# The order of steps in a two-layer, two-stream pipeline: no empty slots, the first layer two tiles ahead of the second, and two buffers for its output

## The chip, the cores and the metric

The kernel runs on one core of one Trainium2 chip. The metric is the device time of that core in microseconds (us). Three runs of the kernel before gave 3565.03, 3568.47 and 3568.79 us; the median is 3568.47 us. The engines are TensorE (PE: matmuls; PEld is its weight load), VectorE (DVE), ScalarE (ACT), GpSimd (POOL), and SyncE (SP), which here issues the DMAs.

## The reference

The input x is 8 sequences of 1024 tokens of 256 features. A layer norm gives xn; the output is x + A(xn) + F(xn). A is a linear attention with a second-order Taylor feature map, and comes first in the program. F is a transformer of two layers, and it is the part that the change touches:

```
for l in range(2):                      # F
    h = shift_token(x)                  # second half of the features from the token before
    q, k, v = split(h @ wqkv[l])        # 8 heads of 64
    q, k = rotary_xpos(l2norm(q) * qs, l2norm(k) * ks)
    o = local_attention(q, k, v)        # windows of 128, each looks at the one before too
    x = x + o @ wo[l]
    h = layer_norm(shift_token(x))
    a, g = split(h @ w1[l] + b1[l])     # 682 each
    x = x + (a * gelu(g)) @ w2[l] + b2[l]
```

Tile `it` of layer 1 needs only tile `it` of layer 0's output and what layer 1 kept of tile `it - 1` (keys, values, one shifted row).

## The kernel before, in words

The Taylor part (`taylor_block`) ends at about 917 us. The rest is `transformer_block`. It treats the 8 sequences as two streams `s` of 4 sequences each; a stream is 32 tiles (`ROUNDS`) of 128 tokens. A **step** is one tile of one layer of one stream, a tuple `(n, s, l, it)`: its number `n` in the order of work, stream, layer and tile. There are 2 x 2 x 32 = 128 steps.

The work runs in **slots**. Slot `j` takes five steps at once, each at another stage of its life, as `steps_at(j)` returns them:

- `nxt` = step at `j + 1`: for a layer-1 step, PE transposes layer 0's output `xmid` (`x_T`) and ACT copies it into `hT` (`copy_hT`); for a layer-0 step nothing, since `hT` is loaded by DMA;
- `cur` = step at `j`: the projections K, Q and V (`project`), norms and rotation, transposes of the heads (`heads_T`), and scores;
- `att` = step at `j - 1`: exponentials, transposes of the probabilities (`prob_T`), `attend`, `out_project`;
- `nrm` = step at `j - 2`: the residual sum `x1` (`add_attention`), the token shift by DMA, the layer norm, `hn_T`;
- `ffn` = step at `j - 3`: `up`, GELU and gate, `down`, and the sum `add_ffn` into `xmid` (layer 0) or `yout` (layer 1).

Each engine has one `slot` function that lists the work of the five stages in a fixed order, and `run` calls it for every slot from -1 to `SLOTS + 2`. Where `steps_at` gives `None`, that stage's work is left out. Engines wait for each other by semaphores which count steps, so the order of steps is what `step_of(j)` says. All loops are unrolled when the program is built.

`step_of` before: slot 0 holds (stream 0, layer 0, tile 0) and slot 2 (stream 1, layer 0, tile 0); slots 1 and 3 are empty. From slot 4 on, four slots make a round `r`: (0, layer 0, tile r), (0, layer 1, tile r-1), (1, layer 0, tile r), (1, layer 1, tile r-1). The last four slots, 128 to 131, are empty, (0, layer 1, tile 31), empty, (1, layer 1, tile 31). That makes 132 slots for 128 steps, and three more (132 to 134) in which the last steps run out. A slot is called *full* here when `cur`, `att`, `nrm` and `ffn` all are there: slot 5 and slots 7 to 127. Each empty slot also leaves a hole in the `att`, `nrm` and `ffn` work of the three slots behind it.

`middle_of(step)` gives the number of the layer-0 step whose output a layer-1 step reads; `x_T` on PE waits for it on the semaphore `x2_ready`.

Names in the profile: `f_ps` is PSUM, L1362 `project`, L1367 `heads_T`, L1389 and L1396 scores, L1407 and L1411 `prob_T`, L1426 and L1436 `attend`, L1447 `out_project`, L1348 and L1349 `x_T`, L1454 `hn_T`, L1470 and L1475 `up`, L1482 `down`, L1170 the copy of the normalised tile `hnT` on DVE, L1103 `unit_k` on DVE. On SP: L917 loads part of `hT` for a layer-0 step, L939 keeps the values of a tile for the next one.

Of the kernel before, what the change touches and what calls it, by code (L numbers as in the profile page):

```python
# [15 lines left out]
ALU = mybir.AluOpType  # L16
# [3 lines left out]
P = 128  # L20
DIM = 256
# [11 lines left out]
SLOTS = 6  # L33
# [673 lines left out]
def transformer_block(nc, PAIRS, x, xn_d, attn_d, xnT_d, wqkv_s, wo, w1, b1, w2, ln, id_s, rot, masks_s, last_stored, out):  # L707
# [6 lines left out]
    with ExitStack() as ctx:  # L714
# [12 lines left out]
        ps = ctx.enter_context(nc.psum_tensor("f_ps", [P, 8, 512], F32))  # L727

        SCORES = (0, 1, 2, 3)
        XT, HNT, K, V, Q, KT, QT, OT, WO, DOWN = 4, 5, 4, 5, 5, 4, 5, 6, 7, 3  # L730
# [12 lines left out]
        def per_stream(name, shape):  # L743
            return [sb(f"{name}{s}", shape) for s in range(2)]

        xin = per_stream("xin", [P, DIM])
# [3 lines left out]
        vw = per_thread("vw", [P, 4, INNER])  # L750
        x1 = per_thread("x1", [P, DIM + P])
        xsh = per_thread("xsh", [P, P])
        xmid = per_stream("xmid", [P, DIM])
        yout = per_stream("yout", [P, DIM])
        xb = per_stream("xb", [P, DIM])
        qk = sb("qk", [P, 2 * HEADS, HD])
# [37 lines left out]
        xT_ps = sem("xT_ps")  # L794
# [37 lines left out]
        x1_ready = sem("x1_ready")  # L832
# [18 lines left out]
        STREAMS = range(2)  # L851
        PAIRS_OF_HEADS = [(0, 2), (1, 3), (4, 6), (5, 7)]
        MIDDLE, OWN, OLDEST, NEWEST = range(4)
        ROUNDS = PAIRS * TILES
        SLOTS = 4 * ROUNDS + 4
        block = ctx.enter_context(nc.Block())

        def thread_step(r, c):

            r, c = r + c // 4, c % 4  # L860
            return 4 * r + c - 2, c // 2, c % 2, r - c % 2

        def step_of(j):
            if j in (0, 2):
                return j // 2, j // 2, 0, 0
            if j < 4 or j >= SLOTS or j in (SLOTS - 4, SLOTS - 2):
                return None
            if j >= SLOTS - 4:
                return 4 * ROUNDS - 2 + (j - SLOTS + 3) // 2, (j - SLOTS + 3) // 2, 1, ROUNDS - 1
            return thread_step(j // 4, j % 4)  # L870

        FIRST_FFN = 3

# [13 lines left out]
            return not isinstance(count, int) or count > 0  # L887

        def middle_of(step):

            n, s, l, it = step
            if isinstance(it, int) and it in (0, ROUNDS - 1):
                return s if it == 0 else 4 * ROUNDS - 6 + 2 * s
            return n - 5

        def chances(h):
            k = h // 2 % 2
# [173 lines left out]
        def _(dve):  # L1071
# [61 lines left out]

            def add_attention(step):
                n, s, l, it = step
                xprev = xin[s] if l == 0 else xmid[s]
                if l == 0:
                    dve.wait_ge(xn_in[s], 16 * it + 16)
                if some(it):
                    dve.wait_ge(carried[s][l], 16 * it)  # L1140
                dve.wait_ge(wo_ps, n + 1)
                v.tensor_tensor(x1[s][l][:, 0:DIM], ps[:, WO, 0:DIM], xprev[:, :], ALU.add).then_inc(x1_ready, 1)

            def row_statistics(step):
                n, s, l, it = step
# [37 lines left out]
            def add_ffn(step):  # L1183
                n, s, l, it = step
                if l == 0:
                    dve.wait_ge(down_ps, n + 1)
                    v.tensor_tensor(xmid[s][:, :], ps[:, DOWN, 0:DIM], x1[s][l][:, 0:DIM], ALU.add).then_inc(x2_ready, 1)
                else:
                    if some(it):
                        dve.wait_ge(y_out[s], 16 * it)  # L1190
                    dve.wait_ge(xb_ready[s], 2 * it + 2)
                    dve.wait_ge(down_ps, n + 1)
                    v.tensor_tensor(yout[s][:, :], ps[:, DOWN, 0:DIM], xb[s][:, :], ALU.add).then_inc(x2_ready, 1)
# [146 lines left out]
        def _(pe):  # L1340
            mm, tr = nc.tensor.matmul, nc.tensor.transpose

            def x_T(step):
                n, s, l, it = step
                if l == 0:
                    return
                pe.wait_ge(x2_ready, middle_of(step) + 1)
                tr(ps[:, XT, 0:P], xmid[s][:, P:DIM], id_s[:, :])  # L1348
                tr(ps[:, XT, P:2 * P], xmid[s][:, 0:P], id_s[:, :]).then_inc(xT_ps, 1)  # L1349

            def project(step, i, b, done):
                n, s, l, it = step
# [274 lines left out]
```

## Time and profile before

| | |
|---|---|
| runs, us | 3565.03, 3568.47, 3568.79 (median 3568.47) |
| profiled execution, us | 3566.8 |
| its span, first to last instruction, us | 3564.7 |
| mean granted TensorE clock | 0.989 |
| PE matmul busy | 3441.9 us, 97% |
| PE weight load busy | 2425.4 us, 68% |
| DVE / ACT / POOL busy | 2619.5 / 2667.9 / 1332.4 us |
| TensorE's share of the chain that ended last | 71% |

The page shows the span in 40 slices of 89 us with the busy tenths of each engine. The transformer part begins at 922.97 us with the first projection. The stretches that matter are short beside the span (one slot is about 20 us), so they are read from the busy times by stretch and from the timeline, not from the page.

### The profile page before, as it was taken

How to read it: one execution, taken by the hardware profiler on the slowest of the kernel's cores; microseconds unless marked ns; L12 is line 12 of the kernel's file. 1: busy time of each engine (PE TensorE's matmuls, PEld its weight loads, DVE VectorE, ACT ScalarE, POOL GpSimd, SP SyncE). 2: the span in 40 equal slices, each digit the busy share in tenths (PEclk: the TensorE clock that was granted, in tenths of full speed). 3: DMA queues.
4: the chain of work that ended last, by engine and by line, in shares of the span. 5: the costliest groups of instructions: out<-in, count | busy, mean ns of one | idle time of the engine just before them, and what ended most of it. 6: DMA issues, size and time to landing. Idle time of an engine off the chain costs nothing.

```text
span 3564.7 us, 87646 instructions
## 1 busy us (share of the span) xinstructions
PE 3441.9 (97%) x32608; PEld 2425.4 (68%) x32608; DVE 2619.5 (73%) x8000; ACT 2667.9 (75%) x5724; POOL 1332.4 (37%) x1194
## 2 busy tenths in 40 slices
PE   7999999999689999999999999999999999999997
PEld 3433344433468787878788787778788787878786
DVE  3665555654578888888888888888887888888874
ACT  6788877788367777777777777777777777777774
POOL 1221212211244444444444444444444444444432
PEclk9999999999799999999999999999999999999999
DMA  6655675546322222222222222222222222222210
GB/s 156 143 136 128 131 155 135 119 96 112 107 56 68 67 65 72 61 72 63 71 66 70 65 64 73 61 72 63 71 66 68 67 64 73 61 71 64 71 45 22
DMA packets 289671, 293.21 MB, mean 82 GB/s; under 512 B 40928, under 2 KB 221280, under 8 KB 288736
## 3 DMA queue, kind: packets, MB, share of 16 engines
q1 hardware_dynamic: 289248, 287.62, 34.1%
q8 instruction: 260, 4.26, 0.5%
q14 instruction: 163, 1.34, 0.1%
HBM read 104.77 MB, written 58.73 MB: 46 GB/s over the span
## 4 chain that ended last, share of the span: by engine, by line
PE 71%; issue 2%; DVE 1%; POOL 1%; ACT 0%; DMA 0%; SPq 0%; POOLq 0%; DVEq 0%; ACTq 0%
PE f_ps L1362 18%; PE f_ps L1470 16%; PE f_ps L1482 9%; PE f_ps L1447 6%; PE f_ps L1426 4%; PE f_ps L1367 3%; PE f_ps L1389 3%; PE f_ps L1407 3%; PE f_ps L1436 2%; PE f_ps L1396 2%; PE f_ps L1475 2%; PE f_ps L1411 2%; PE f_ps L1454 1%; PE f_ps L1348 0%; POOL turned L1033 0%
## 5 line engine op out<-in xcount | busy, mean ns | idle before, releaser
L1033 POOL TENSOR_TENSOR turned<-qk,rot 128x256 f32<-128x256 f32 x512 | 407.2, 816 | 1287.8 <-ACT qk L1245 1258.8
L1362 PE MATMUL f_ps<-wqkv_s,hT 128*128 128x512 f32 x1536 | 707.2, 596 | 9.5 <-DMA hT<-xnT_dram 5.5
L1470 PEld LDWEIGHTS f_ps<-hnT,w_s 128*128 128x128 f32 x5120 | 596.3, 193 | 70.9 <-issue 61.6
L1470 PE MATMUL f_ps<-hnT,w_s 128*128 128x128 f32 x5120 | 597.7, 276 | 10.3 <-DVE hnT L1170 10.3
L1113 DVE CUSTOM_DVE_ANT_0 pr<-f_ps,masks_s 128x192 f32<-128x192 f32 x1024 | 326.3, 355 | 355.2 <-PE f_ps L1396 353.2
L545 ACT ACTIVATE weights<-t_ps,four_s 128x1024 f32<-128x1024 f32 x576 | 580.4, 1302 | 7.6 <-PE t_ps L653 7.2
L1278 ACT ACTIVATE pr<-pr,nmax,rnorm 128x192 f32<-128x192 f32 x1024 | 545.2, 535 | 46.6 <-DVE nmax L1120 46.6
L1362 PEld LDWEIGHTS f_ps<-wqkv_s,hT 128*128 128x128 f32 x1536 | 276.8, 190 | 276.0 <-issue 188.0
L1130 DVE TENSOR_SCALAR pr<-pr,rsum 128x192 f32<-128x192 f32 x1024 | 439.9, 491 | 9.0
L392 DVE SCALAR_TENSOR_TENSOR weights<-weights,causal_s 128x512 f32<-128x512 f32 x192 | 163.9, 868 | 279.3 <-ACT weights L545 278.9
L1482 PE MATMUL f_ps<-w_s,act_u 128*128 128x256 f32 x1536 | 352.7, 379 | 0.0
L670 PE MATMUL t_ps<-weights,vals 128*32 128x512 f32 (+3 forms) x3072 | 308.6, 497 | 18.4 <-DVE weights L392 13.1
L653 PE MATMUL t_ps<-qkT 96*128 96x512 bf16 (+3 forms) x1536 | 308.9, 332 | 13.7 <-ACT weights L545 8.0
L1040 POOL TENSOR_TENSOR rnorm<-ssq,f_mhalf 128x8 f32<-128x8 f32 x128 | 254.5, 1988 | 159.5 <-DVE ssq L1090 159.5
L1482 PEld LDWEIGHTS f_ps<-w_s,act_u 128*128 128x128 f32 x1536 | 281.9, 190 | 33.5 <-issue 0.5
L1267 ACT ACTIVATE kT<-f_ps 128x512 f32<-128x512 f32 x128 | 76.4, 597 | 295.9 <-PE f_ps L1367 295.9
L653 PEld LDWEIGHTS t_ps<-qkT 96*128 96x128 bf16 x1536 | 111.7, 98 | 272.7 <-ACT weights L545 174.9
L1302 ACT ACTIVATE act_u<-f_ps,b_s 128x128 f32<-128x128 f32 x640 | 205.1, 365 | 112.3 <-PE f_ps L1475 89.1
L286 POOL TENSOR_TENSOR yT<-yT,den 128x1024 f32<-128x1024 f32 x24 | 62.8, 2615 | 539.7 <-DVE den L335 539.7
L1447 PE MATMUL f_ps<-fwo_s,oT 128*128 128x256 f32 x1024 | 242.8, 380 | 2.7 <-ACT oT L1291 2.6
L1080 DVE TENSOR_TENSOR cosine<-qk,rot 128x512 f32<-128x512 f32 x256 | 208.9, 816 | 20.1 <-ACT qk L1245 19.9
L1180 DVE SCALAR_TENSOR_TENSOR act_u<-f_ps,b_s,act_u 128x128 f32<-128x128 f32 (+1 forms) x768 | 208.8, 340 | 17.7 <-ACT act_u L1302 13.5
(119 smaller groups left out, 6312.6 us busy)
## 6 DMA issues: line engine op xcount, KB each, us to landing
vw<-vw SPq DMA_DIRECT2D x628, 128.0 KB, 2.5
qkT<-parts_dram SPq DMA_DIRECT2D x384, 128.0 KB, 5.8
kT<-kT SPq DMA_DIRECT2D x124, 256.0 KB, 2.7
parts_dram<-parts SPq DMA_DIRECT2D x64, 384.0 KB, 2.9
xnT_dram<-xnT SPq DMA_DIRECT2D x8, 1025.0 KB, 4.8
xs<-x_dram SPq DMA_DIRECT2D x8, 1024.0 KB, 7.9
xn_dram<-xn SPq DMA_DIRECT2D x8, 1024.0 KB, 5.4
attn_dram<-ao SPq DMA_DIRECT2D x8, 1024.0 KB, 10.5
```

The lines of the kernel that those rows point to most:

```text
L545: a.activation(weights[:, w:w + 2, :], ps[:, bank:bank + 2, :], ACT.Square, bias=four_s[:, :]).then_inc(squared, 1)
L653: last = mm(ps[:, unit_bank(n) + k, o:o + 512 - c], qkT[g % 2][:, 1, h, j * P:(j + 1) * P], qkT[g % 2][:, 0, h, half * 512 + c:(half + 1) ...
L670: last = mm(ps[h * VP:(h + 1) * VP, half, c:512], vals[:, j, g * GH + h, :], weights[:, GH * (i % RING) + h, o:o + 512 - c], start=(j == 0 ...
L1033: g.tensor_tensor(turned[:, heads, f], qk[:, heads, z], sines, ALU.mult).then_inc(done, 1)
L1040: g.tensor_tensor(rnorm[:, HEADS:], ssq[:, HEADS:], mhalf[:, HEADS:], ALU.pow).then_inc(knorm_ready, 1)
L1113: last = v.tensor_tensor_reduce(out=chances(h), in0=ps[:, SCORES[p], k * 256:k * 256 + BAND], in1=mask_of(it)[:, HALF - k * HALF:HALF - k ...
L1130: last = v.tensor_scalar_mul(chances(h), chances(h), rsum[:, h:h + 1])
L1278: last = a.activation(chances(h), chances(h), ACT.Exp, bias=nmax[:, h:h + 1], scale=rnorm[:, h:h + 1], accum_out=psum[:, h:h + 1])
L1362: last = mm(ps[:, b, :], rows, wqkv_s[:, l, c, i * INNER:(i + 1) * INNER], start=(c == 0), stop=(c == KC - 1))
L1447: last = mm(ps[:, WO, 0:DIM], oT[:, c, :], wo_s[:, l, c, :], start=(c == 0), stop=(c == INNER // P - 1))
L1470: last = mm(ps[:, UP[j // 2], o:o + P], w1_s[:, l, c, half * FULL + j * P:half * FULL + j * P + P], hnT[:, c, :], start=(c == 0), stop=(c ...
L1482: last = mm(ps[:, DOWN, 0:DIM], act_u[:, j, :], w2_s[:, l, j, :], start=(j == 0), stop=(j == FB - 1))
```

## The change

`step_of` becomes a lookup in a list, `ORDER`, with 128 entries for 128 slots. The list begins with layer 0 of tiles 0 and 1 of both streams, and then alternates layer 0 of tile r + 2 with layer 1 of tile r; for the last two tiles only layer 1 is left. So the order is (stream, layer, tile): (0,0,0), (1,0,0), (0,0,1), (1,0,1), (0,0,2), (0,1,0), (1,0,2), (1,1,0), ... , (0,1,30), (1,1,30), (0,1,31), (1,1,31). Since layer 0 is now two tiles ahead, its output `xmid` has two buffers per stream, picked by `it % 2`. In the middle a stream's step of one layer still comes four slots after that layer's step before it. At the start three such pairs have a distance of two slots (slots 0 and 2, 1 and 3, 2 and 4) and one has three (3 and 6); at the end three have two (123 and 125, 124 and 126, 125 and 127) and one has three (121 and 124).

```diff
-        xmid = per_stream("xmid", [P, DIM])
+        xmid = per_stream("xmid", [P, 2, DIM])
...
-        SLOTS = 4 * ROUNDS + 4
+        SLOTS = 4 * ROUNDS
...
-        def thread_step(r, c):
-
-            r, c = r + c // 4, c % 4
-            return 4 * r + c - 2, c // 2, c % 2, r - c % 2
+        AHEAD = 2
+        ORDER = [(s, 0, it) for it in range(AHEAD) for s in STREAMS]
+        for r in range(ROUNDS):
+            for s in STREAMS:
+                if r + AHEAD < ROUNDS:
+                    ORDER.append((s, 0, r + AHEAD))
+                ORDER.append((s, 1, r))
+        NUMBER = {step: n for n, step in enumerate(ORDER)}
 
         def step_of(j):
-            if j in (0, 2):
-                return j // 2, j // 2, 0, 0
-            if j < 4 or j >= SLOTS or j in (SLOTS - 4, SLOTS - 2):
-                return None
-            if j >= SLOTS - 4:
-                return 4 * ROUNDS - 2 + (j - SLOTS + 3) // 2, (j - SLOTS + 3) // 2, 1, ROUNDS - 1
-            return thread_step(j // 4, j % 4)
+            return (j,) + ORDER[j] if 0 <= j < SLOTS else None
...
         def middle_of(step):
-
             n, s, l, it = step
-            if isinstance(it, int) and it in (0, ROUNDS - 1):
-                return s if it == 0 else 4 * ROUNDS - 6 + 2 * s
-            return n - 5
+            return NUMBER[s, 0, it]
...
-                xprev = xin[s] if l == 0 else xmid[s]
+                xprev = xin[s][:, :] if l == 0 else xmid[s][:, it % 2, :]
...
-                    v.tensor_tensor(xmid[s][:, :], ps[:, DOWN, 0:DIM], x1[s][l][:, 0:DIM], ALU.add).then_inc(x2_ready, 1)
+                    v.tensor_tensor(xmid[s][:, it % 2, :], ps[:, DOWN, 0:DIM], x1[s][l][:, 0:DIM], ALU.add).then_inc(x2_ready, 1)
...
-                tr(ps[:, XT, 0:P], xmid[s][:, P:DIM], id_s[:, :])
-                tr(ps[:, XT, P:2 * P], xmid[s][:, 0:P], id_s[:, :]).then_inc(xT_ps, 1)
+                tr(ps[:, XT, 0:P], xmid[s][:, it % 2, P:DIM], id_s[:, :])
+                tr(ps[:, XT, P:2 * P], xmid[s][:, it % 2, 0:P], id_s[:, :]).then_inc(xT_ps, 1)
```

The line numbers of the changed kernel are 5 lower behind `middle_of` (L1362 becomes L1357, and so on).

On PE, behind the scores of the very first step, the kernel before has the whole attention of that step by itself (`prob_T`, `attend`, `out_project`), and then the projections of the next one:

```order
L1407 MATMUL f_ps<-id_s,pr 128x128 x8
L1411 MATMUL f_ps<-id_s,pr 128x128 x4
L1426 MATMUL f_ps<-pT,vw 64x128 x8
L1436 MATMUL f_ps<-pT,vw 64x64 x16
L1447 MATMUL f_ps<-fwo_s,oT 128x256 x4
L1362 MATMUL f_ps<-wqkv_s,hT 128x512 x6
L1367 MATMUL f_ps<-id_s,qk 128x128 x8
```

At the same place on PE the changed kernel has the projections of the second step first, and the attention of the first step among its transposes and scores:

```order
L1357 MATMUL f_ps<-wqkv_s,hT 128x512 x6
L1402 MATMUL f_ps<-id_s,pr 128x128 x8
L1406 MATMUL f_ps<-id_s,pr 128x128 x4
L1362 MATMUL f_ps<-id_s,qk 128x128 x8
L1421 MATMUL f_ps<-pT,vw 64x128 x8
L1431 MATMUL f_ps<-pT,vw 64x64 x16
L1384 MATMUL f_ps<-kT,qT 64x128 x4
L1391 MATMUL f_ps<-kT,qT 64x64 x4
```

The second step has moved up by one slot, so that slot 1 holds the two steps' work together; the third step (tile 1 of stream 0) follows in slot 2, and from slot 3 on every slot is full.

The last rows of PE in the kernel before: `up`, attention and `down` of slot 132, and then the last step's `hn_T`, `up` and `down` with no other work between:

```order
L1470 MATMUL f_ps<-hnT,w_s 128x128 x20
L1475 MATMUL f_ps<-hnT,w_s 106x128 x2
L1407 MATMUL f_ps<-id_s,pr 128x128 x8
L1411 MATMUL f_ps<-id_s,pr 128x128 x4
L1482 MATMUL f_ps<-w_s,act_u 128x256 x6
L1426 MATMUL f_ps<-pT,vw 64x128 x8
L1436 MATMUL f_ps<-pT,vw 64x64 x16
L1447 MATMUL f_ps<-fwo_s,oT 128x256 x4
L1454 MATMUL f_ps<-id_s,hn 128x128 x2
L1470 MATMUL f_ps<-hnT,w_s 128x128 x20
L1475 MATMUL f_ps<-hnT,w_s 106x128 x2
L1482 MATMUL f_ps<-w_s,act_u 128x256 x6
```

The last rows of PE in the changed kernel, from the `down` of slot 128 on (L1421 and L1431 are `attend`, L1449 `hn_T`, L1442 `out_project`, L1465 and L1470 `up`, L1477 `down`):

```order
L1477 MATMUL f_ps<-w_s,act_u 128x256 x6
L1421 MATMUL f_ps<-pT,vw 64x128 x8
L1431 MATMUL f_ps<-pT,vw 64x64 x16
L1449 MATMUL f_ps<-id_s,hn 128x128 x2
L1442 MATMUL f_ps<-fwo_s,oT 128x256 x4
L1465 MATMUL f_ps<-hnT,w_s 128x128 x20
L1470 MATMUL f_ps<-hnT,w_s 106x128 x2
L1477 MATMUL f_ps<-w_s,act_u 128x256 x6
L1449 MATMUL f_ps<-id_s,hn 128x128 x2
L1465 MATMUL f_ps<-hnT,w_s 128x128 x20
L1470 MATMUL f_ps<-hnT,w_s 106x128 x2
L1477 MATMUL f_ps<-w_s,act_u 128x256 x6
```

Between the last `out_project` and the last `hn_T` there now stand an `up` and a `down` of the step before.

## Rows read from the trace of the kernel before

**Rows 1.** The page: span, busy time of PE, and its 40 slices
```profile
span 3564.7 us, 87646 instructions
PE   7999999999689999999999999999999999999997
```

**Rows 2.** Busy time by stretch (us, busy and count per engine, clock, DMA): slots 7 to 126
```profile
1038.20:3444.00 2405.80, 2405.68 (x25321) 1930.62 (x25320) 1980.70 (x6600) 1821.04 (x4441) 1066.56 (x960) 1.00 0.26 67
```

**Rows 3.** Groups by line, the same stretch (busy, mean ns, idle before): projections
```profile
L1362 PE MATMUL f_ps<-wqkv_s,hT 128*128 128x512 f32 x1440 | 660.1, 594 | 0.1
```

**Rows 4.** Busy time by stretch: slots 0 to 6, one row each
```profile
922.97:940.40 17.43, 12.90 (x84) 7.28 (x84) 6.86 (x15) 4.56 (x9) 10.43 (x16) 0.70 0.97 361
940.40:952.10 11.70, 7.00 (x68) 5.56 (x69) 4.43 (x25) 6.52 (x20) 0.00 (x0) 0.66 0.33 83
952.10:966.80 14.70, 10.56 (x87) 5.91 (x85) 9.11 (x27) 5.10 (x11) 7.49 (x7) 0.84 0.15 37
966.80:983.90 17.10, 13.94 (x125) 12.86 (x125) 6.68 (x29) 8.92 (x25) 0.00 (x0) 0.84 0.17 42
983.90:999.50 15.60, 11.45 (x89) 6.97 (x87) 9.60 (x29) 6.29 (x12) 7.54 (x7) 0.78 0.17 43
999.50:1019.50 20.00, 19.93 (x208) 15.87 (x209) 14.51 (x50) 15.91 (x42) 7.04 (x6) 1.00 0.21 51
1019.50:1038.20 18.70, 14.69 (x158) 10.41 (x157) 13.91 (x50) 11.06 (x31) 8.02 (x7) 0.91 0.24 60
```

**Rows 5.** Busy time by stretch: slots 128 to 132, then the last step alone
```profile
3464.10:3478.80 14.70, 13.10 (x129) 11.84 (x129) 7.99 (x33) 8.78 (x24) 0.56 (x1) 1.00 0.19 50
3478.80:3495.30 16.50, 15.65 (x144) 11.90 (x142) 11.12 (x29) 7.61 (x15) 10.16 (x9) 1.00 0.11 31
3495.30:3513.20 17.90, 14.36 (x128) 13.07 (x128) 7.57 (x34) 10.47 (x29) 0.00 (x0) 0.90 0.08 22
3513.20:3527.50 14.30, 10.19 (x85) 6.25 (x83) 9.30 (x22) 5.77 (x10) 8.91 (x9) 0.81 0.10 24
3527.50:3544.10 16.60, 13.52 (x134) 11.55 (x127) 7.51 (x34) 9.76 (x27) 0.00 (x0) 0.96 0.03 9
3544.10:3551.80 7.70, 0.69 (x2) 0.29 (x2) 3.64 (x9) 0.00 (x0) 1.97 (x3) 0.84 0.03 8
3551.80:3564.70 12.90, 9.79 (x56) 9.13 (x56) 2.24 (x7) 1.99 (x6) 0.00 (x0) 0.83 0.03 10
```

**Rows 6.** Timeline of PE (start, us, instructions, idle before): slots 0 and 6
```profile
922.97 6.12 PE L1362 MATMUL f_ps<-wqkv_s,hT 128*128 128x512 f32 x8 [5.52 <-DMA hT<-xnT_dram]
...
1019.50 3.60 PE L1362 MATMUL f_ps<-wqkv_s,hT 128*128 128x512 f32 x8
1024.12 1.98 PE L1362 MATMUL f_ps<-wqkv_s,hT 128*128 128x512 f32 x4 [1.03 <-ACT qk L1245]
...
1030.40 1.97 PE L1367 MATMUL f_ps<-id_s,qk 128*128 128x128 f32 x8 [2.98 <-DVE qk L1103]
```

**Rows 7.** Timeline of SP's queue and of PE in slots 0 and 3
```profile
934.25 0.45 SPq L917 DMA_DIRECT2D hT<-xnT_dram  x1
...
969.27 6.12 PE L1470 MATMUL f_ps<-hnT,w_s 128*128 128x128 f32 x40 [2.44 <-DVE hnT L1170]
```

**Rows 8.** One line's instructions (L917, up to 1000 us): its loads' landings
```profile
DMA to landing us min/median/max: 2.0/2.5/9.6
```

**Rows 9.** One line's instructions (L939, 1100 to 3000 us): its copies' landings
```profile
DMA to landing us min/median/max: 2.2/2.6/4.1
```

**Rows 10.** Timeline of PE in the last slots
```profile
3530.65 4.73 PE L1470 MATMUL f_ps<-hnT,w_s 128*128 128x128 f32 x40 [2.34 <-DVE hnT L1170]
...
3550.34 0.69 PE L1454 MATMUL f_ps<-id_s,hn 128*128 128x128 f32 x2 [6.26 <-DVE hn L1162]
...
3551.85 6.76 PE L1470 MATMUL f_ps<-hnT,w_s 128*128 128x128 f32 x40 [0.82 <-DVE hnT L1170]
...
3558.88 2.76 PE L1482 MATMUL f_ps<-w_s,act_u 128*128 128x256 f32 x12
```

More of the change, by code:

```diff
@@ L1141, in add_attention @@
                 dve.wait_ge(wo_ps, n + 1)
-                v.tensor_tensor(x1[s][l][:, 0:DIM], ps[:, WO, 0:DIM], xprev[:, :], ALU.add).then_inc(x1_ready, 1)
+                v.tensor_tensor(x1[s][l][:, 0:DIM], ps[:, WO, 0:DIM], xprev, ALU.add).then_inc(x1_ready, 1)
             def row_statistics(step):
```

## The prediction, made before the changed kernel had run

> **What bounds the kernel now.** I read the page first, for where PE is not busy; then the busy times by stretch; then the timeline at both ends of the transformer part. The page shows 9 or more tenths of PE in nearly every slice. The exceptions are the first slice, two around the start of the transformer part (6 and 8 tenths), and the last [rows 1]. In between, from 1038.2 to 3444.0 us, PE has matmuls for 2405.68 of 2405.80 us, at a granted clock of 1.00, while DVE is busy for 1980.70 and ACT for 1821.04 us [rows 2]. In that stretch 1440 projection matmuls ran [rows 3]; a step has 12 of them (8 for K and Q, 4 for V, as slot 6 shows them [rows 6]), so it is 120 slots of 2405.8 / 120 = 20.05 us. PE's own work sets the full slot; nothing else ends late there.
>
> At the ends it is otherwise. Slots 0 to 6 have 90.5 us of PE work in 115.2 us, and in all but the full slot 5 the granted clock was only 0.66 to 0.91 [rows 4]. The stretches behind slot 127 have 77.3 us in 100.6 us [rows 5]. There the waits are chains between engines: PE idles 2.98 us in slot 6 until DVE has the unit keys, and 6.26 us before the last `hn_T` [rows 6, 10]. So 24.7 us of idle time lie at the start and 23.3 at the end. The two stretches do the work of 128 - 121 = 7 full slots, 140.3 us, and have 167.8 us of PE busy for it: the other 27.5 us are matmuls at the lower clock. Together 75 us; the rest of the transformer part has no idle time to give.
>
> **The change part by part.** It removes no arithmetic: 128 steps before and after, with the same instructions each. It changes how many slots are full. The sum goes over the whole transformer part, from 922.97 us to the end of the span at 3564.7 us.
>
> Before: slots 0 to 6 take 17.43 + 11.70 + 14.70 + 17.10 + 15.60 + 20.00 + 18.70 = 115.2 us [rows 4]; slots 7 to 127 take 3464.1 - 1038.2 = 2425.9 us, 121 slots of 20.05; and what follows takes 14.7 + 16.5 + 17.9 + 14.3 + 16.6 + 7.7 + 12.9 = 100.6 us [rows 5]. The total is 2641.7 us.
>
> After, slot by slot:
>
> Slot 0 is as before, 17.4 us. It has one step's `cur` work, and it begins when its DMA lands [rows 6].
>
> Slot 1 has `cur` of the second step and `att` of the first. The trace has no such slot. From above it is bounded by nothing overlapping: slot 1 of before, which is that attention alone, and slot 2, which is that `cur` alone, 11.7 + 14.7 = 26.4 us [rows 4]. From below it is bounded by PE never idle: slot 6 holds the same matmuls and a few transposes more, and has 14.7 us of PE work [rows 4]; less half a microsecond for those, 14.2 us. The nearest row is slot 6 itself, 18.7 us: it has `cur`, `att` and `nrm` and no `ffn`. Its critical part is from the K projection at 1019.50 to the transposes of the heads at 1030.40, 10.9 us [rows 6], through ACT, POOL and DVE, and that chain doesn't change in slot 1. I take 18.7 less 1.0 us for the work of `nrm` that isn't there: 17.7 us.
>
> Here the clock matters. Slot 0's eight K and Q matmuls took 6.12 us against 3.60 in slot 6, and the clock granted over slots 0 and 1 was 0.70 and 0.66 of the upper level, a mixture of 1.2 and 2.4 GHz [rows 4, 6]. In slot 1 of before PE had idled about 3 us before the first transposes; in the changed kernel it goes from the scores straight to projections. If the lower level lasted through K and Q, slot 1 would be 2.5 us longer, 20.2 us; the bounds above hold either. The Trainium skill, "TensorE: Matmul & The Clock Gate", section "What's actually happening", says that the throttled state is the default and that activity releases it. By that rule the busier slot 1 gets the upper level early and the 17.7 us stand; by slot 0's row alone it would be 20.2 us. The trace agrees with the rule in that all 120 full slots had 1.00.
>
> Slot 2 has `cur`, `att` and `nrm` and no `ffn`, exactly as slot 6: 18.7 us, and not under its 14.7 us of PE work. From slot 3 on all slots are full, to slot 127: 125 slots of 20.05 = 2506.1 us. The order of kinds in them (stream 0 layer 0, stream 0 layer 1, stream 1 layer 0, stream 1 layer 1) is that of before for slots 4 to 123, so every engine's list in a slot is the same, SP's and POOL's too. `x_T` had no wait in any full slot of before (PE's idle sum is 0.12 us), and now its input is four slots older. Slots 0 to 4 hold five layer-0 steps in a row and slots 123 to 127 five layer-1 steps; their PE work differs only by `x_T`, which was in the mean.
>
> Behind slot 127: slot 128 has `att`, `nrm` and `ffn`, as slot 128 had before: 14.7 us, less the `x_T` that it had, 14.4. Slot 129 has `nrm` of the last step beside `ffn` of the one before. `up` and `down` are 4.9 and 2.6 us at full clock (in slot 132 `up` ran in 4.73 with its 0.4 of edge rows behind it, `down` is 2.76 and overlaps [rows 10]); together with gates in between I take 8.3 us. The chain that gives the last `hn`, 6.3 us in the row of 3550.34, runs beside it and is hidden. Its ends are 7.5 us (PE alone) and 7.5 + 6.3 = 13.8 us (nothing hidden). Slot 130 is the last `ffn`: from `hn_T` at 3550.34 to the end it took 14.4 us, with `up` at the lower clock (6.76 us against 4.73 in slot 132 [rows 10]). Before, PE had idled 6.26 us ahead of it, and now it comes straight from `down`, so I take the upper level: 14.4 - 2.0 - 0.3 = 12.1 us, and 14.4 us as the other end.
>
> The sum: 17.4 + 17.7 + 18.7 + 2506.1 + 14.4 + 8.3 + 12.1 = 2594.7 us, against 2641.7: 47.0 us less. The span would be 3517.7 us and the profiled execution (2.1 us above its span) 3519.8 us. The profiled execution of before, 3566.8 us, is 1.7 us under the median of the runs, so for the median I expect 3568.5 - 47.0 = 3521.5, say 3522 us.
>
> The second `xmid` buffer costs nothing in time: the same instructions with another offset. The first layer-0 tiles want their DMAs sooner, while the weights still load. The last `hT` load of the third step was issued at 934.25 us and landed at most 9.6 us later [rows 7, 8], by 944 us; PE wants it at the start of slot 2, at 922.97 + 17.4 + 17.7 = 958 us. It is hidden by 14 us, and the loads of `w1` and `w2` that `up` waits for in slot 3 had landed before too, as PE's `up` in slot 3 of before started at 969.27 us and waited for DVE's `hnT` and not for them [rows 7]; its place is now 976.8 us or later.
>
> **What the distance of two could cost.** At both ends a thread's step follows its predecessor by two slots in place of four. What the next step needs from the one before are kept keys, kept values and the carried row. The values are the tightest: SP issues them behind `attend`, which in a full slot ends some 16 us in, they land 2.6 us later in the median and at most 4.1 [rows 9], three copies; ACT's copy of the next V comes about 10 us into the slot after. That leaves some 8 us. Queued behind such a wait would be ACT's copies of the probabilities, and behind them PE's `attend`. I cost it at nothing, and at 5 us for each of the six pairs at a distance of two if SP is late by being stuck in front of another wait.
>
> **The rivals.**
>
> *Close pairs wait.* Six times 5 us: 3522 + 30 = 3552 us. For it: SP's queue is in order and it waits for `hn_ready` and `v_ready` before it reaches the values. Against: all of these come earlier in the slot than `attend`.
>
> *Less overlap at the ends.* Slot 1 at 22, slot 129 at 12 and the last `up` at the lower clock: 4.3 + 3.7 + 2.3 = 10 us more, 3532 us. This is the forecast with its unknown terms near the upper ends.
>
> *Slower: the full slot gets longer.* PE is at 1.00 of the clock for 2406 us, and no empty slot interrupts it in that stretch. If PE, now dense from slot 1 to slot 129, were granted a lower clock, the price is on 125 slots: at 0.98, 20.05 / 0.98 = 20.46, or 51 us in all, and the time would be 3573 us. The point from which it decides is 47 / 125 = 0.38 us a slot, a granted clock of 0.981. Against it speaks that the clock never fell in 120 full slots in a row [rows 2]; five more won't differ.
>
> *The change doesn't do what it says.* It gains at one end only, because the other has a chain that I don't see. Idle time and lower clock are split about evenly between the ends (24.7 and 23.3 us idle), so one end alone gives half of 47 us: 3545 us. For it: slots 1 and 2 are not in the trace as they will be. Against: slots 6, 128 and 132 are nearly the new slots 2, 128 and 129.
>
> **How the numbers follow.** The forecast, 3522 us, has 0.80; its own range is 3515 to 3530. Less overlap at the ends, 3532 us, has 0.10. Close pairs or one end only, 3545 to 3552 us, have 0.04 and 0.02. The slower clock has 0.02. About 0.02 are left for a reason that makes no difference in all. A measurement of this kernel can tell about 0.2%, 7 us, from no change. All cases but the last two are faster by more than that: faster 0.96, same 0.02, slower 0.02. The lower end of the range is from the bounds: slot 1 at 14.2 and slot 2 at 14.7 would take 7.5 us off, so 3514.5; the upper end takes in the 3532 us case. The range is 3515 to 3534 us.
>
> **What would show it.** In the changed kernel's profile, from the first projection: slot 3 should begin 53.8 us in, with its predecessors at 17.4, 17.7 and 18.7 us. The 125 full slots should have a mean of 20.05 us with no idle time of PE and a clock of 1.00. From the end of the last scores (start of slot 128) to the end of the span it should be 35 us, and the wait before the last `hn_T` under 1 us where it was 6.26. If close pairs wait, ACT's copy of V or PE's `attend` shows idle time in slots 2 to 5 or 124 to 127. The prediction is wrong if the full slots' mean moves by more than 0.05 us, or if one end doesn't shrink.

## The result and the profile after

| | before | after |
|---|---|---|
| runs, median (range), us | 3568.07 (3565.03 to 3568.79) | 3518.58 (3517.42 to 3520.59) |
| profiled execution, us | 3566.8 | 3517.4 |
| its span, us | 3564.7 | 3515.6 |
| mean granted TensorE clock | 0.989 | 0.995 |

The ratio is 0.9865, with a 95% interval of 0.9853 to 0.9876: 49.5 us less. Two later sets of runs of the same kernel gave 0.9869 (0.9854 to 0.9884) and 0.9870 (0.9854 to 0.9887), which is 46.2 us (3567.55 to 3521.38) and 47.2 us (3567.90 to 3520.72). The forecast was 3522 us, its range 3515 to 3534.

The page of the changed kernel, span, PE and granted clock in 40 slices:

```profile
span 3515.6 us, 87647 instructions
PE   7999999999699999999999999999999999999999
PEclk9999999999899999999999999999999999999999
```

Against [rows 1], one low slice is left near the start of the transformer part where there were two, and the last slice has 9 tenths where it had 7.

The busy time of the engines by stretch (us; busy time and count of PE, PEld, DVE, ACT, POOL; clock; DMA share; GB/s). The rows are slot 0, slot 1, slot 2, slots 3 to 127, slot 128, slot 129 up to `hn_T`, and the rest:

```profile
922.22:938.13 15.91, 11.13 (x84) 6.18 (x85) 6.67 (x15) 4.49 (x9) 10.32 (x16) 0.82 0.97 361
938.13:955.42 17.29, 13.31 (x157) 8.91 (x153) 12.95 (x48) 11.64 (x33) 7.02 (x6) 0.98 0.46 115
955.42:973.79 18.37, 14.36 (x156) 10.08 (x155) 13.63 (x49) 10.63 (x29) 8.01 (x7) 0.91 0.24 60
973.79:3481.10 2507.31, 2506.98 (x26379) 2011.18 (x26377) 2061.30 (x6877) 1896.87 (x4631) 1107.85 (x999) 1.00 0.26 66
3481.10:3495.89 14.79, 12.97 (x127) 11.65 (x127) 8.21 (x33) 8.13 (x22) 1.98 (x3) 1.00 0.05 15
3495.89:3503.39 7.50, 7.50 (x58) 7.14 (x57) 3.52 (x13) 1.98 (x6) 1.96 (x3) 1.00 0.04 10
3503.39:3515.60 12.21, 8.14 (x59) 7.24 (x57) 3.30 (x10) 1.98 (x6) 0.00 (x0) 1.00 0.06 21
```

These rows answer to [rows 2, 4, 5]. The account of the transformer part:

| stretch | before | forecast | after |
|---|---|---|---|
| slots that fill the pipeline | 115.2 (0 to 6) | 53.8 (0 to 2) | 51.6 |
| full slots | 2425.9 (121 of 20.05) | 2506.1 (125 of 20.05) | 2507.3 (125 of 20.06) |
| behind slot 127 | 100.6 | 34.8 | 34.5 |
| sum | 2641.7 | 2594.7 | 2593.4 |

The sum fell by 48.3 us; the other 0.8 us of the span's 49.1 are ahead of it, in the Taylor part that the change doesn't touch: the first projection started at 922.22 and not at 922.97 us. PE's idle time in the full slots is 0.33 us in 2507. In the two ends PE's idle time fell from 48.0 us (24.7 and 23.3) to 18.7 us (86.1 us less 67.4 busy). What the ends take over the pure work of 128 slots (128 x 20.05 = 2566.4 us) fell from 75 to 27 us, so the rest of the gain, some 19 us, is shorter busy time of PE for the same work: matmuls that no longer run at the lower clock level.

What became of the chain ahead of the last `hn_T` is in the timeline (start, us, instructions, idle time before and what ended it). PE runs `up` and `down` of the step before, DVE normalises the last tile beside them:

```profile
3495.89 4.63 PE L1465 MATMUL f_ps<-hnT,w_s 128*128 128x128 f32 x40
...
3499.19 0.29 DVE L1146 BATCH_NORM_STATS2 st<-xsh 128x6 f32<-128x128 f32 x1 [2.26 <-DMA xsh<-x]
...
3500.80 2.76 PE L1477 MATMUL f_ps<-w_s,act_u 128*128 128x256 f32 x12
...
3502.55 0.33 DVE L1157 TENSOR_SCALAR hn<-xsh,mv,rstd 128x128 f32<-128x128 f32 x1
3503.39 0.38 PE L1449 MATMUL f_ps<-id_s,hn 128*128 128x128 f32 x2
...
3504.80 4.73 PE L1465 MATMUL f_ps<-hnT,w_s 128*128 128x128 f32 x40 [1.03 <-DVE hnT L1165]
```

The last half of `hn` is done at 3502.88 us, half a microsecond before PE is free for it. The 6.26 us of idle time of [rows 10] are gone, and the last `up` runs in 4.73 us, at the upper clock level, where it took 6.76.

The waits of ACT (who waited for whom: us in total, times, longest) show what the close pairs cost, first in slots 3 to 127, then in slots 0 to 2:

```profile
ACT kT L1262 <- PE f_ps L1362: 284.3, 125, 2.6
ACT vw L1255 <- PE f_ps L1357: 129.6, 125, 1.3
...
ACT kT L1262 <- PE f_ps L1362: 8.8, 3, 3.3
ACT vw L1255 <- PE f_ps L1357: 4.2, 3, 1.4
```

The copies of K and V waited for PE in all 128 steps, never for a DMA that keeps the keys or values of the step before. The first close pair is slots 0 and 2. SP issues the last of its three copies of values in slot 1, and ACT's copy of the next V stands in slot 2:

```profile
953.74 0.60 SPq L936 DMA_DIRECT2D vw<-vw  x1
...
962.12 0.60 ACT L1255 ACTIVATE vw<-f_ps 128x512 f32<-128x512 f32 x1 [1.41 <-PE f_ps L1357]
```

The three copies of this line up to 1000 us landed at most 3.6 us after issue, so by 957.3 us at the latest: nearly 5 us in hand, where the prediction had estimated some 8.

### The profile page after: what moved, and what is told of

It is laid out like the page before. It is cut to its first block, busy times and chain, and to the rows that moved or that the text cites. A ratio compares the mean times of both kernels' runs of the same rounds, so it can differ in the third digit from the quotient of the medians.

```text
span 3515.6 us, 87647 instructions
## 1 busy us (share of the span) xinstructions
PE 3421.8 (97%) x32608; PEld 2412.3 (69%) x32608; DVE 2617.1 (74%) x8000; ACT 2663.9 (76%) x5724; POOL 1330.7 (38%) x1194
## 3 DMA queue, kind: packets, MB, share of 16 engines
q1 hardware_dynamic: 289248, 287.62, 34.8%
## 4 chain that ended last, share of the span: by engine, by line
PE 72%; DVE 1%; POOL 0%; ACT 0%; issue 0%; DMA 0%; SPq 0%; DVEq 0%; POOLq 0%
PE f_ps L1357 18%; PE f_ps L1465 16%; PE f_ps L1477 9%; PE f_ps L1442 6%; PE f_ps L1421 4%; PE f_ps L1362 3%; PE f_ps L1384 3%; PE f_ps L1402 3%; PE f_ps L1431 2%; PE f_ps L1391 2%; PE f_ps L1470 2%; PE f_ps L1406 2%; PE f_ps L1449 1%; PE f_ps L1343 0%; DVE pr L1108 0%
## 5 line engine op out<-in xcount | busy, mean ns | idle before, releaser
L1357 PE MATMUL f_ps<-wqkv_s,hT 128*128 128x512 f32 x1536 | 706.8, 595 | 9.4 <-DMA hT<-xnT_dram 5.6
L1465 PEld LDWEIGHTS f_ps<-hnT,w_s 128*128 128x128 f32 x5120 | 591.7, 192 | 63.0 <-issue 59.8
L1465 PE MATMUL f_ps<-hnT,w_s 128*128 128x128 f32 x5120 | 592.5, 275 | 2.5 <-DVE hnT L1165 2.5
L1357 PEld LDWEIGHTS f_ps<-wqkv_s,hT 128*128 128x128 f32 x1536 | 276.7, 190 | 273.8 <-issue 186.0
L1477 PE MATMUL f_ps<-w_s,act_u 128*128 128x256 f32 x1536 | 352.7, 379 | 0.0
L1477 PEld LDWEIGHTS f_ps<-w_s,act_u 128*128 128x128 f32 x1536 | 281.9, 190 | 33.0
L1442 PE MATMUL f_ps<-fwo_s,oT 128*128 128x256 f32 x1024 | 242.4, 380 | 0.3 <-ACT oT L1286 0.3
## 6 DMA issues: line engine op xcount, KB each, us to landing
attn_dram<-ao SPq DMA_DIRECT2D x8, 1024.0 KB, 10.3
```

What stands on the lines that cost most here:

```text
L1357: last = mm(ps[:, b, :], rows, wqkv_s[:, l, c, i * INNER:(i + 1) * INNER], start=(c == 0), stop=(c == KC - 1))
L1442: last = mm(ps[:, WO, 0:DIM], oT[:, c, :], wo_s[:, l, c, :], start=(c == 0), stop=(c == INNER // P - 1))
L1465: last = mm(ps[:, UP[j // 2], o:o + P], w1_s[:, l, c, half * FULL + j * P:half * FULL + j * P + P], hnT[:, c, :], start=(c == 0), stop=(c ...
L1477: last = mm(ps[:, DOWN, 0:DIM], act_u[:, j, :], w2_s[:, l, j, :], start=(j == 0), stop=(j == FB - 1))
```

## The experiments

All were compared with the kernel before on the same chip. The changed kernel itself ran again beside the last five of them, not beside the first four; those are set against its 3518.6 us of the result. There it took 3521.38 and 3520.72 us, both within what had been expected (3518.6 within 3 us, and 3517 to 3523). Two theories stood against each other. **Holes**: an empty slot costs what PE idles and what clock it loses in it and in the three slots behind, whose work is missing by turns; nothing else in the change moves time. **Lead**: the two tiles of distance, or the second buffer, take a wait away. Three helpers stand in the edits: `PLACED` is `ORDER` with empty slots, and `step_of(j)` looks a step up in it; `NUMBER` gives its number as before.

### Holes back at the end, start dense

```diff
-        SLOTS = 4 * ROUNDS
+        SLOTS = 4 * ROUNDS + 2
...
+        PLACED = ORDER[:-2] + [None, ORDER[-2], None, ORDER[-1]]
```

> The changed kernel (two ahead, two buffers) with two empty slots put back before each of the last two steps, as before had them; the start stays dense. Theory (the time is in the holes): start as in the changed kernel, 51.6 us for slots 0 to 2, then 123 full slots of 20.06, then 100.6 us as the kernel before had behind slot 127: 2619 us against 2593, so 3518.6 + 26 = 3545 us. Rival (the lead of two tiles or the second buffer brings the gain, holes cost nothing because the engines drain at the same pace): 3519 us.

Measured: 3549.46 us (3548.11 to 3550.48), ratio 0.9955 (0.9940 to 0.9970). Its stretches: fill, 123 full slots, and the rest.

```profile
922.21:978.28 56.07, 44.11 (x390) 28.71 (x391) 33.36 (x109) 26.73 (x69) 25.46 (x29) 0.80 0.51 162
978.28:3445.34 2467.06, 2466.73 (x25955) 1978.67 (x25953) 2028.27 (x6767) 1866.26 (x4555) 1087.82 (x981) 1.00 0.26 66
3445.34:3547.40 102.06, 78.70 (x665) 65.34 (x664) 49.90 (x166) 44.40 (x110) 23.10 (x24) 0.88 0.11 29
```

The end is 102.1 us long, where before had 100.6, and the full slots keep their 20.06 us. The lead is there in full and brings nothing. The median was 4 us over the expected 3545 us; in the profile that is the fill, 56.1 us against 51.6, at a granted clock of 0.80. The same instructions stand in those slots: PE is busy for 44.1 us in place of 38.8. The later runs return to this.

### Holes back at the start, end dense

```diff
-        SLOTS = 4 * ROUNDS
+        SLOTS = 4 * ROUNDS + 2
...
+        PLACED = [ORDER[0], None, ORDER[1], None] + ORDER[2:]
```

> The changed kernel with two empty slots put back behind each of the first two steps, as before had them; the end stays dense. Theory: 115.2 us for slots 0 to 6, 123 full slots of 20.06, 34.5 us behind the last full slot: 2617 us, so 3542 us. Rival (lead or buffer): 3519 us. With the other run: the two losses must add up to the whole gain of 49 us, if start and end are independent.

Measured: 3541.85 us (3539.45 to 3542.56), ratio 0.9932 (0.9916 to 0.9949).

```profile
922.27:1037.00 114.73, 89.79 (x810) 64.21 (x811) 64.49 (x217) 57.52 (x141) 40.62 (x43) 0.83 0.33 100
1037.00:3504.10 2467.10, 2466.61 (x25960) 1979.66 (x25958) 2031.26 (x6771) 1868.33 (x4559) 1094.90 (x985) 1.00 0.26 66
3504.10:3538.60 34.50, 28.81 (x240) 26.08 (x240) 14.72 (x56) 11.80 (x33) 3.95 (x6) 1.00 0.05 16
```

The start is nearly that of before (115.2 us), the end that of after (34.5 us). Against 3518.6 us the two losses are 30.9 and 23.3 us, 54.2 us together where the whole gain is 49.5. The 4.7 us too many are about the 4.5 us by which the fill was longer in the profile of the run with end holes. The stretches leave that out. The end holes add 102.1 - 34.5 us and take two full slots away: 27.4 us. The start holes give 114.7 - 51.6 less two full slots: 23.0 us. That is 50.5 us together against the 48.3 of the account above, so they add up within about 2 us, and the end's part is the larger.

### Old order, two buffers

```diff
-        xmid = per_stream("xmid", [P, DIM])
+        xmid = per_stream("xmid", [P, 2, DIM])
```

(and `it % 2` in its four uses; nothing else. The order is that of the kernel before.)

> The kernel before with the second xmid buffer and nothing else of the change (order with four empty slots, one tile ahead). Theory: the buffer by itself moves nothing, 3568 us, full slot 20.05 us. Rival (the buffer frees a wait between the layers, or its shift of the addresses behind it changes durations): away from 3568 by more than 7 us.

Measured: 3566.71 us (3561.71 to 3567.71) against 3565.44 for before in the same set; ratio 1.000 (0.9991 to 1.001). The busy times over the 120 slots of [rows 2]:

```profile
1037.98:3443.90 2405.92, 2405.81 (x25321) 1930.58 (x25320) 1981.76 (x6600) 1821.16 (x4441) 1065.96 (x960) 1.00 0.26 67
```

A slot is 2405.92 / 120 = 20.05 us, as it was. The buffer alone does nothing; it only allows the order.

### One buffer, one tile ahead, two holes

```diff
-        xmid = per_stream("xmid", [P, 2, DIM])
+        xmid = per_stream("xmid", [P, 1, DIM])
...
+        AT = {}
+        for it in range(ROUNDS):
+            for s in STREAMS:
+                AT[4 * it + 2 * s - 1 if it else s] = (s, 0, it)
+                AT[min(4 * it + 4, 4 * ROUNDS - 1) + 2 * s] = (s, 1, it)
+        PLACED = [AT.get(j) for j in range(SLOTS)]    # SLOTS = 4 * ROUNDS + 2
```

> One xmid buffer and layer 0 one tile ahead as before, in the densest order that this allows: slots 0 and 1 hold the first two layer-0 steps, slot 2 is empty, then the alternation, and slot 129 behind (0,1,31) is empty, 130 slots. Theory (a hole costs about 12 us wherever it is, the lead nothing): two holes remain of four, some 100 us at the start to slot 5, 122 full slots, 68.5 us at the end: 2616 us, 3541 us. Rival (the lead of two tiles is what helps): near 3568 us.

Measured: 3544.27 us (3543.92 to 3545.49), ratio 0.9941 (0.9926 to 0.9956). So the step `(0,1,31)` stands in slot 127, the hole behind it is slot 128, and the last step is in slot 129. Fill, 122 full slots, rest:

```profile
920.25:1025.20 104.95, 87.75 (x814) 61.88 (x815) 65.36 (x220) 57.97 (x145) 41.35 (x43) 0.88 0.36 108
1025.20:3471.11 2445.91, 2445.69 (x25743) 1962.60 (x25741) 2014.10 (x6710) 1851.62 (x4516) 1084.62 (x976) 1.00 0.26 66
3471.11:3542.60 71.49, 54.06 (x453) 46.38 (x452) 32.90 (x112) 28.32 (x73) 14.13 (x15) 0.90 0.07 18
```

Two holes fewer than before give 21 us (3565.44 less 3544.27; 19 us by the stretches of the two traces), with the old lead and one buffer: not quite half of the gain. The median is 3 us over the expected 3541 us; the start took 105.0 us where some 100 were expected, and the end 71.5 where 68.5 were. What the second buffer buys is the other two holes, some 26 us (3544.27 less 3518.58).

### A hole in the middle

```diff
-        SLOTS = 4 * ROUNDS
+        SLOTS = 4 * ROUNDS + 1
...
+        PLACED = ORDER[:64] + [None] + ORDER[64:]
```

> The changed kernel with one empty slot put in behind step 63, in the middle of the full slots. Theory (an empty slot costs what PE idles in it and in the three slots behind, whose work is missing by turns, and the clock that it loses there): four holes cost 49 us at the ends, so about 12 us, 3531 us. Rival (in the middle the engines catch up, since PE alone is the bound and the others have a quarter of their time free, and the cost belongs to start and end): under 4 us, 3521 us.

Measured: 3530.73 us (3528.63 to 3533.98); the changed kernel in the same set 3521.38 us. The stretches are slot 63, the hole, the three slots behind it, and the next:

```profile
2178.56:2198.65 20.09, 20.08 (x211) 15.84 (x209) 16.68 (x56) 15.23 (x39) 10.17 (x9) 1.00 0.25 65
2198.65:2213.38 14.73, 12.92 (x126) 11.65 (x127) 8.15 (x33) 8.07 (x21) 0.56 (x1) 1.00 0.30 80
2213.38:2230.06 16.68, 15.83 (x145) 12.09 (x143) 11.35 (x29) 7.91 (x17) 10.16 (x9) 1.00 0.12 32
2230.06:2251.17 21.11, 20.12 (x210) 15.88 (x210) 15.49 (x57) 16.30 (x42) 7.04 (x6) 1.00 0.24 61
2251.17:2270.99 19.82, 15.81 (x157) 11.38 (x156) 13.85 (x50) 11.01 (x31) 8.01 (x7) 0.83 0.29 70
2270.99:2290.91 19.92, 19.92 (x211) 16.02 (x210) 16.52 (x55) 15.06 (x38) 10.17 (x9) 1.00 0.19 51
```

The four slots take 72.3 us for the work of three (60.2 us): 12.2 us for one hole. PE idles for 7.7 us of them (1.8, 0.9, 1.0 and 4.0 us in the four slots), and the other 4.5 us are longer busy time for the same work, 3.4 of them in the last slot, at 0.83 of the clock. The medians differ by 9.4 us and the spans of the two profiles by 10.3: the fill of this run was 3.3 us shorter than that of the changed kernel beside it (52.65 us at 0.87 against 55.90 at 0.80), and its first projection came 1.5 us later. The rival's 4 us is out: the engines do not catch up. The most expensive slot is the last, 19.8 us with no `ffn` in it. PE's work there would be 12.4 us at the upper clock (a full slot's 19.9 less 7.5 of `up` and `down`); it is busy for 15.8 because the granted clock fell to 0.83, and nothing fills the wait for the keys, which ended here:

```profile
2262.07 1.97 PE L1364 MATMUL f_ps<-id_s,qk 128*128 128x128 f32 x8 [2.98 <-DVE qk L1100]
```

An empty slot isn't 20 us lost, nor nothing: it shifts work out of four slots, and in each the chain between the engines is longer than what PE has left.

### Three tiles ahead

```diff
-        AHEAD = 2
+        AHEAD = 3
```

(with three `xmid` buffers and `it % 3`; `xb` moved to other memory to make room.)

> Layer 0 three tiles ahead with three xmid buffers (xb moved to the memory of a table no longer used, to make room), no empty slots. Theory (only holes cost): as the changed kernel, 3519 us within 2 us, since all slots from 3 to 127 are full here too; twice as many pairs of steps follow at a distance of two, and they cost nothing. Rival (pairs at a distance of two wait, or the lead itself helps): away from 3519 us by more than 4 us, slower with idle time of PE in slots 2 to 9 and 118 to 127, or faster.

Measured: 3520.17 us (3517.13 to 3521.79); the changed kernel in the same set 3521.38 (3518.90 to 3523.37). Fill, 125 full slots, rest:

```profile
920.95:973.60 52.65, 40.10 (x390) 26.16 (x391) 33.26 (x109) 26.74 (x69) 25.41 (x29) 0.87 0.52 168
973.60:3480.89 2507.29, 2507.01 (x26379) 2011.24 (x26377) 2061.10 (x6877) 1897.18 (x4631) 1109.88 (x999) 1.00 0.26 66
3480.89:3515.30 34.41, 28.55 (x240) 26.02 (x240) 14.93 (x56) 11.98 (x33) 3.94 (x6) 1.00 0.05 16
```

More lead and more close pairs change nothing that can be measured, in the total, the full slots or the end. The pairs at a distance of two are 10 here (five at either end) against 6 (three at either end), and not twice as many as the text before the run says. The fill of 52.7 us lies between the 51.6 and 55.9 us of the changed kernel's profiles, with the same instructions.

### First loads early

```diff
+                if b + 1 == B:      # in store_attn, ahead of the Taylor part's last store, on SP
+                    for s in range(2):
+                        hT, hT_in = first_hT[s]
+                        rows = xnT_d[s * (B // 2)]
+                        sp.wait_ge(xnT_stored, 16 * (s * (B // 2) + 1))
+                        sp.dma_start(hT[:, 0:P], rows[1, :, 0:P]).then_inc(hT_in, 16)
+                        sp.dma_start(hT[:, P + 1:2 * P + 1], rows[0, :, 1:1 + P]).then_inc(hT_in, 16)
...
-            for s in STREAMS:
-                load_hT(s, 0)
```

> The changed kernel, with the two streams' first hT loads issued at the end of the Taylor part, ahead of its last store, in place of the first thing in the transformer part. PE now idles 5.6 us before the first projection, from the Taylor part's last matmul to the load's landing. Theory (what is left of the gain at the start is the fill, so an earlier first projection moves all behind it): about 3 to 4 us of the 5.6 go, 3515 us. Rival (slot 0 then waits for something else, zeroing by GpSimd or the start of the block): 3518.6 us as the changed kernel.

Measured: 3517.13 us (3514.72 to 3518.72) against 3521.38 for the changed kernel in the same set; ratios to before 0.9859 (0.9843 to 0.9875) and 0.9869 (0.9854 to 0.9884). PE's first projection in its timeline:

```profile
915.47 5.37 PE L1362 MATMUL f_ps<-wqkv_s,first_hT 128*128 128x512 f32 x8 [1.37 <-PEq L62]
```

The wait of 5.6 us became 1.4 us, and the medians differ by the same 4 us. The intervals overlap, so the total alone doesn't prove it; the wait's going is plain in the trace. The fill itself is as it was (55.56 us at 0.82, against 55.90 at 0.80). The 3515 us expected are missed by 2.1 us, as the changed kernel beside it was 2.8 us above the 3518.6 that they were reckoned from.

### PE kept busy in the fill

```diff
+            def keep_warm(count):
+                for _ in range(count):
+                    tr(ps[:, WO, 3 * P:4 * P], id_s[:, :], id_s[:, :])
...
+                if cur and cur[0] == 0:
+                    keep_warm(20)
                 if cur:
                     project(cur, 1, K, k_ps)
...
+                if cur and cur[0] < 3:
+                    keep_warm(14)
                 if cur:
                     pe.wait_ge(k_unit, cur[0] + 1)
```

> The changed kernel with idle-time transposes of the identity on TensorE, into columns of PSUM that nobody reads: 20 ahead of the first projection, while it waits for its load, and 14 ahead of the transposes of the heads in slots 0, 1 and 2, where PE waits about 3 us for VectorE. The three slots of the fill took 51.6 us at a mean granted clock of 0.91 in one run of the changed kernel and 55.9 us at 0.69 to 0.87 in another, with all else equal. Theory (what varies in the fill, and 4 to 9 us of its length, is the clock that PE loses in these waits): the fill's clock goes to 0.95 or more, its length to 46 to 49 us, and the median to about 3514 us, with runs closer together. Rival (the fill is bound by the chain through ScalarE, GpSimd and VectorE, and the extra transposes only get in its way): 3519 to 3524 us.

Measured: 3514.10 us (3511.78 to 3516.02); the changed kernel in the same set 3520.72 (3518.72 to 3522.97). Ratios to before 0.9852 (0.9838 to 0.9867) and 0.9870 (0.9854 to 0.9887). The fill, slots 0 to 2, in one stretch, first of this kernel:

```profile
919.26:968.14 48.88, 40.46 (x432) 27.37 (x433) 33.26 (x109) 26.79 (x69) 25.39 (x29) 0.97 0.55 177
```

Then of the changed kernel, in the profile of its second set of runs, slot by slot, and last its three slots in one stretch in the set of this experiment:

```profile
920.98:938.51 17.53, 13.00 (x85) 7.28 (x85) 6.79 (x15) 4.49 (x9) 10.41 (x16) 0.69 0.99 364
938.51:957.23 18.72, 15.19 (x157) 10.16 (x154) 12.94 (x48) 11.62 (x33) 7.02 (x6) 0.87 0.31 75
957.23:976.88 19.65, 15.64 (x155) 11.20 (x154) 13.62 (x49) 10.62 (x29) 8.01 (x7) 0.83 0.26 65
...
922.50:978.14 55.64, 43.47 (x391) 28.58 (x392) 33.35 (x109) 26.74 (x69) 25.43 (x29) 0.80 0.51 163
```

With 42 transposes more in it, and 20 ahead of it, the fill is 48.9 us at a mean granted clock of 0.97. Without them it was 51.6 us in the first profile of the changed kernel (0.91; 0.82, 0.98 and 0.91 in its slots), 55.9 in the second and 55.6 in the third (both 0.80). Three more kernels of these experiments have the same three slots untouched: 56.1 us at 0.80 with the end holes, and 52.65 at 0.87 both with three tiles ahead and with the hole in the middle. In these six PE's idle time is 12.0 to 12.8 us, and its busy time runs from 38.8 to 44.1 us. So what varies in the untouched fill is how long the matmuls take, with the clock. The transposes take from both: against the third profile idle time fell from 12.2 to 8.4 us and busy time from 43.5 to 40.5, though it holds more work. The chain through the other engines isn't held up by it.

No run of this kernel was as slow as the fastest of the changed kernel beside it (3516.02 against 3518.72), though the intervals of the ratios overlap. Of the 9.9 us between the two profiles' spans the fill explains 6.8. The rest lies in the Taylor part: its last matmul ended at 913.7 us in this profile and at 916.9 in the other, with the same instructions, and the first projection followed 5.5 and 5.6 us later. So the medians' 6.6 us agree with the fill, and the forecast of 3514 us with a fill of 46 to 49 us came out. The runs did not come closer together, as had been expected, but stayed 4.2 us apart with and without the transposes; the end of the Taylor part, which lies between 913.7 and 917.4 us in the profiles, varies as much by itself.

### Both

The two edits above together, with 8 transposes ahead of the first projection in place of 20.

> The same idle-time transposes on top of the early first loads (8 ahead of the first projection, as the wait there is short). Theory: both savings add, since one is ahead of slot 0 and the other in it: 4 to 5 us earlier first projection and 4 to 9 us less fill, about 3510 us. Rival: 3517 us as with the early loads alone.

Measured: 3514.38 us (3513.70 to 3514.88), ratio 0.9853 (0.9839 to 0.9868). They don't add up; the forecast of 3510 us was wrong. The start of the transformer part and the fill in its profile:

```profile
918.37 1.78 PE L1487 MATMUL f_ps<-id_s 128*128 128x128 f32 x8 [1.37 <-PEq L62]
919.94 4.61 PE L1362 MATMUL f_ps<-wqkv_s,first_hT 128*128 128x512 f32 x8
...
919.94:970.90 50.96, 42.91 (x433) 28.73 (x433) 35.22 (x109) 26.86 (x69) 26.79 (x37) 0.91 0.55 178
```

Two things are missing. With the early loads alone the projections began 1.37 us behind the Taylor part; here the eight transposes stand in that place, and the projections begin 1.6 us later. And the fill is 2 us longer than with the warm fill alone, at 0.91 of the clock: the first eight projection matmuls took 4.61 us here, 3.70 with twenty transposes ahead of them, and 5.37 with none and the early loads. That eight were too few for the clock fits this, but isn't shown, since one profile each is all there is. Twenty take the projections' place for longer still (2.4 us in the run above); with early loads they weren't tried. Both kernels, the warm fill and this one, have medians under the changed kernel's.

## Why the prediction was right

**PE sets the full slot, and the order doesn't change it.** Forecast 125 slots of 20.05 us; measured 20.06, and 20.05 to 20.06 in every order tried: one, two or three tiles ahead, with one, two or three buffers. One word of the text before the prediction needs setting right: slot 5 of the kernel before isn't full, since its `nrm` would be the step of the empty slot 3 (its row has 208 matmuls, a full slot 211). The sum doesn't hang on it, as slots 0 to 6 entered it as measured.

**The time lies in the ends.** Start and end holes each put their share back. The prediction took 47.0 us for the four holes; 48.3 came in the profile, and 49.5, 46.2 and 47.2 in the medians of three sets of runs. One hole in the middle costs 12.2 us in its trace, a quarter of that.

**Slot 1**, which no row of before showed, was set at 17.7 us from slot 6 less the work of `nrm`; it took 17.3, and 18.7 and 18.6 in the profiles of the later sets. The bounds of 14.2 and 26.4 us were far wider than needed. Slot 2 was set at 18.7 us and took 18.4, and 19.7 and 19.6 later.

**Slot 0** was taken as before, 17.4 us, and took 15.9. Here the term was no constant: in the later sets it took 17.5 and 17.4 with the same instructions. The prediction treated one sample of the clock at the start as the value. So the fill, forecast at 53.8 us, came out 2.2 us under in the first profile and some 2 us over in the two others: that it looks so near in each slot of the first is in part luck, and the forecast lies in the middle of what this stretch does. In slot 1 the eight K and Q matmuls, which take 3.60 us at the upper level and had taken 6.12 in slot 0 of before, ran so:

```profile
938.13 3.98 PE L1357 MATMUL f_ps<-wqkv_s,hT 128*128 128x512 f32 x8
```

In the later profiles they took 4.39 and 4.29 us: 0.4 to 0.8 us over the upper level, where the prediction's other case had 2.5. The Trainium skill, "TensorE: Matmul & The Clock Gate", section "What's actually happening", has activity release the throttle; by that rule slot 1 was to stay at 17.7 us, by slot 0's row to be 20.2. The granted clock of slot 1 was 0.98 in the first profile (17.3 us) and 0.87 in the second (18.7 us), and the run with the most transposes had 0.97 over the fill. The traces agree with the rule, but a dense order alone doesn't make its effect certain.

**The end**: slot 128 14.4 us forecast, 14.8 measured; slot 129 8.3 and 7.5, because PE had no gap between `up` and `down`; the last `ffn` 12.1 and 12.2. The chain that gives the last `hn` is hidden as stated, with half a microsecond to spare, and the last `up` ran at the upper level.

**The rivals.** That close pairs wait: refuted by the waits of ACT, which name PE in all 128 steps, and by three tiles ahead, with 10 such pairs in place of 6. That the full slot would lose clock: 1.00 over 2507 us. That only one end gains: both do, 23 us at the start and 27 at the end. Less overlap at the ends, 3532 us: slot 129 came out under the forecast in the first profile, and slots 1 and 2 at most 1.0 us over it in any, where this rival had 4.3 for slot 1.

## What to carry to other kernels

In a software pipeline over stages, an empty slot costs, in each of the slots that lack a stage, the difference between the chain and the work that is left, and what the matmul engine's clock loses there: here 12 us per hole of a 20 us slot. Count the holes of the order first; they are found in the program and priced from the slots that the trace already has with the same stages missing. A buffer is worth what order it allows, and nothing by itself. When a stretch of 50 us is bound by waits between engines, take its time from more than one profile, because the clock of the matmul engine there differs from run to run.

## What the runs showed of the hardware

The same three slots, with the same instructions, took 51.6, 52.65 (twice), 55.6, 55.9 and 56.1 us in six profiles, at mean granted clocks of 0.91, 0.87 (twice), and 0.80 (three times). TensorE's idle time in them stayed at 12.0 to 12.8 us, its busy time went from 38.8 to 44.1. The last 34.4 to 34.5 us of the kernels with the dense end (the changed kernel, three tiles ahead, the start holes), at 1.00 in all of them, did not vary. Matmuls whose results nobody reads, put in PE's waits, made the stretch shorter (48.9 us at 0.97) although PE had 42 transposes more to do in it. One hole among full slots at 1.00 brought the clock down to 0.83 in the third slot behind it and nowhere else.
